# A projection split over two half cycles of the first batch, and two block turns moved behind an emptying, in a two-layer attention and experts kernel

## The reference, cut to what matters

```python
qz_u = qz @ ternary_factor_u.T * SCALE          # 16 channels x 64
qz_v = qz @ ternary_factor_v.T * SCALE
message_F = einsum('bcsr,bctr->bcst', qz_u, qz_v)
qh = sigmoid(message_F)
qh_v1 = einsum('bcst,bctr->bcsr', qh, qz_v)     # output 0
qh_v2 = einsum('bcst,bcsr->bctr', qh, qz_u)     # output 1
message_G = (qh_v1 @ ternary_factor_u + qh_v2 @ ternary_factor_v) * SCALE
```

## Time and profile before

| | |
|---|---|
| median of 3 runs | 1441.76 us (1440.23 to 1442.63) |
| the profiled execution's own time | 1442.26 us |
| its span in the trace | 1440.1 us (2.2 us lie around it) |
| granted TensorE clock, mean | 0.99 |
| half cycles of batch 0 | 154.9 to 288 us |
| batches 1 to 7 | 288 to 1387 us, some 157 us each |
| last second layer alone | 1387 to 1440 us |

### The profile page before, as it was taken

How to read it: one execution, slowest core, us unless ns; L and a number is a source line. 1 busy time by engine, 2 the same in 40 slices (tenths; PEclk the granted TensorE clock), 3 DMA queues, 4 the chain that set the end, 5 groups by cost and what they waited for, 6 DMA issues and landing times.

```text
span 1440.1 us, 24389 instructions
## 1 busy us (share of the span) xinstructions
PE 1379.7 (96%) x7814; PEld 788.6 (55%) x7814; DVE 897.1 (62%) x1546; ACT 697.7 (48%) x1077; POOL 44.7 (3%) x41
## 2 busy tenths in 40 slices
PE   5989899999999999999999999999999999999977
PEld 3556554455565555555655556555555555555544
DVE  7868544556656566566556565665655665656657
ACT  6556554454444553454535545445445444454431
POOL 4000400000000000000000000000000000000000
PEclk9999999999999999999999999999999999999988
DMA  6012122222112221111222112211122211222110
GB/s 211 1 31 68 37 37 30 30 38 31 26 26 35 36 31 29 33 32 29 30 31 35 32 26 30 39 33 28 24 37 38 30 26 24 35 30 30 27 26 8
DMA packets 298256, 50.66 MB, mean 35 GB/s; under 512 B 276192, under 2 KB 296416, under 8 KB 298112
## 3 DMA queue, kind: packets, MB, share of 16 engines
q1 hardware_dynamic: 297776, 47.29, 19.4%
q0 software_dynamic: 336, 1.64, 0.3%
HBM read 11.64 MB, written 4.19 MB: 11 GB/s over the span
## 4 chain that ended last, share of the span: by engine, by line
issue 85%; PE 2%; DVE 1%; POOL 1%; ACT 0%; POOLq 0%; DVEq 0%
PE psum L1264 2%; DVE arena L925 0%; POOL v_w_hl L614 0%; POOL u_w_hl L614 0%; DVE arena L923 0%; DVE arena L931 0%; POOL rstd_s L629 0%; ACT arena L1035 0%; PE psum L1626 0%; DVE xn_s L669 0%; POOL u_w_hl L611 0%; POOL v_w_hl L611 0%; POOL up_hl L614 0%; DVE x_all L940 0%; POOL gate_hl L611 0%
## 5 line engine op out<-in xcount | busy, mean ns | idle before, releaser
L1203 ACT ACTIVATE arena<-psum 128x1024 f32<-128x1024 f32 x504 | 477.0, 1031 | 611.0 <-PE psum L1264 604.0
L1264 PE MATMUL psum<-arena 128*64 128x512 f32 x2016 | 462.2, 601 | 4.8 <-ACT arena L1203 4.8
L1264 PEld LDWEIGHTS psum<-arena 128*64 128x64 f32 x2016 | 133.9, 137 | 264.8 <-issue 244.3
L1264 PE MATMUL psum<-v_parts,u_parts 64*128 64x512 f32 (+1 forms) x1568 | 208.3, 402 | 12.8 <-DVE o_hl L876 12.6
L1264 PE MATMUL psum<-u_parts,v_parts 64*128 64x512 f32 x1536 | 196.3, 399 | 4.0 <-issue 3.3
L1264 PEld LDWEIGHTS psum<-v_parts,u_parts 64*128 64x128 f32 (+1 forms) x1568 | 144.1, 185 | 101.3 <-issue 58.3
L1264 PEld LDWEIGHTS psum<-u_parts,v_parts 64*128 64x128 f32 x1536 | 139.8, 184 | 84.1 <-issue 39.9
L874 DVE TENSOR_SCALAR o_hl<-psum,sums 128x512 fp32r<-128x512 f32 x126 | 93.5, 742 | 83.3 <-PE psum L1264 82.2
L876 DVE SCALAR_TENSOR_TENSOR o_hl<-psum,sums,o_hl 128x512 fp32r<-128x512 f32 x126 | 94.6, 751 | 4.5
L931 DVE TENSOR_TENSOR arena<-psum,arena 128x512 f32<-128x512 f32 x96 | 64.5, 689 | 50.4 <-PE psum L1264 48.4
L1148 ACT ACTIVATE arena<-psum 128x512 f32<-128x512 f32 x128 | 77.3, 628 | 18.3 <-PE psum L1264 18.3
(11 more groups left out here) (214 smaller groups left out, 1515.2 us busy)
## 6 DMA issues: line engine op xcount, KB each, us to landing
arena<-blocks SPq DMA_DIRECT2D x1008, 32.0 KB, 2.0
x_all<-in_x SPq DMA_DIRECT2D x4, 512.0 KB, 6.1
upper<-in_we SPq DMA_DIRECT2D x8, 256.0 KB, 2.7
expert_rows<-upper SPq DMA_DIRECT2D x16, 128.0 KB, 2.5
xn_s<-expert_rows SPq DMA_DIRECT2D x8, 256.0 KB, 2.9
out<-x_all SPq DMA_DIRECT2D x8, 256.0 KB, 2.8
arena<-in_e POOLq DMA_DIRECT2D x1, 896.0 KB, 6.5
arena<-in_wi POOLq DMA_DIRECT2D x1, 576.0 KB, 6.7
```

The lines of the kernel that those rows point to most:

```text
L1203: nc.scalar.activation(th_of(un), psum[:, at:at + 2], ACT.Tanh, scale=0.5 * FACTOR_SCALE ** 2).then_inc(s_th, 2)
L1264: return nc.tensor.matmul(out, lhsT, rhs, start=start, stop=stop)
```

## The change: what it does

Two things are changed. First, in batch 0 the projection `pj` (six matmuls in even half cycle `2j`, of both outputs of pair `j-1`) becomes two: `pj0` (three matmuls, output 0 of pair `j` itself) in odd half cycle `2j+1`, for pairs 1 to 6, and `pj1` (three matmuls, output 1 of pair `j-1`) in even half cycle `2j`, for pairs 2 to 7. Each has its own bank and its own `add_g`, so DVE adds 12 times in batch 0 where it added 6 times. The last pair of batch 0 is projected whole in batch 1, as before. Counts of semaphores follow (`projected_count`).

Second, from batch 1 on, `turn` of pairs 0 and 2 stands behind `evac_o` of the same even half cycle (0 and 4), not ahead of it.

```diff
+LATE_TURNS = (0, 2)
 def first_middle_of(h):
 
-    work = [w for w in MIDDLE[h] if w[0] in ("pu", "pv", "pj") and w != ("pj", 1)]
-    return work + [("sc", 0)] * (h == FIRST_SCATTER_HALF)
+    j = h // 2
+    if h % 2 == 0:
+        return [("pu", j), ("pv", j)] + [("pj1", j)] * (j > 1)
+    return [("pj0", j)] * (j < PAIRS - 1) + [("sc", 0)] * (h == FIRST_SCATTER_HALF)
+
+
+def projected_count(kind, g):
+
+    return g + PAIRS - 2 if kind == "pj" else g * 2 - (kind == "pj1")
...
+def summed_count(g, o):
+
+    if isinstance(g, int) and g < PAIRS:
+        return projected_count("pj1", g) if o else projected_count("pj0", g - 1)
+    return projected_count("pj", g)
...
-                    dve.wait_ge(s_pj_full, g)
+                    dve.wait_ge(s_pj_full, summed_count(g, o))
...
-                    if o == 0:
+                    late = second and j in LATE_TURNS
+                    if o == 0 and not late:
                         if not some_before:
                             for n in range(2):
                                 dve.wait_ge(s_ymv[n], 16 * E)
                         turn(i, j)
                     evac_o(g, j, o, some_before)
+                    if o == 0 and late:
+                        turn(i, j)
...
-            def project(g, j, bk):
-
-                pe.wait_ge(s_oe, g * 2)
-                was = (j - 1) % PAIRS
-                passes = [(o, a, b) for o in range(2) for a, b in ((0, 0), (0, 1), (1, 0))]
+            def project(kind, g, j, bk):
+
+                pe.wait_ge(s_oe, g * 2 + 1 if kind == "pj0" else g * 2)
+                of = j if kind == "pj0" else (j - 1) % PAIRS
+                outputs = {"pj": (0, 1), "pj0": (0,), "pj1": (1,)}[kind]
+                passes = [(o, a, b) for o in outputs for a, b in ((0, 0), (0, 1), (1, 0))]
...
-                        elif kind == "pj":
-                            if isinstance(i, int) and i == 0 and j == 2:
+                        elif kind in ("pj", "pj0", "pj1"):
+                            if kind == "pj0" and j == 1:
                                 pe.wait_ge(s_parts, 4)
```

More of the change, by code:

```diff
@@ L194 @@
 FIRST_USER_BEFORE = users_before(bank_order(list(FIRST_MIDDLE.items()), 0), False)
+def summed_count(g, o):
+    if isinstance(g, int) and g < PAIRS:
+        return projected_count("pj1", g) if o else projected_count("pj0", g - 1)
+    return projected_count("pj", g)
 def is_prep(work):
-    return work[0] in ("pu", "pv", "pj", "sc")
+    return work[0] in ("pu", "pv", "pj", "pj0", "pj1", "sc")
 def prep_index(g, k):
@@ L853, in _, with add_g @@
             expert_rows(E - 1, 1, E // 2 - 1)
-            def add_g(i, j):
-                bk = x_bank(("pj", j), not (isinstance(i, int) and i == 0))
-                dve.wait_ge(s_pj_full, i * PAIRS + j)
-                if isinstance(i, int) and i == 0 and j == 2:
+            def add_g(i, j, kind):
+                bk = x_bank((kind, j), kind == "pj")
+                dve.wait_ge(s_pj_full, projected_count(kind, i * PAIRS + j))
+                if (kind, j) == ("pj0", 1):
                     dve.wait_ge(s_pj_free, 1)
@@ L863, in add_g @@
                     before = gT[:]
-                if isinstance(i, int) and i == 0 and j == 3:
+                if (kind, j) == ("pj1", FIRST_SCATTER_HALF // 2 + 1):
                     dve.wait_ge(s_scf, 1)
@@ L980, in iteration @@
                 if not attn:
-                    add_g(i, 0)
+                    add_g(i, 0, "pj")
                     for step in L1_STEPS:
@@ L1000, in iteration @@
                             prep_v(g, (j + 1) % 2)
-                        elif work[0] == "pj":
-                            add_g(i, j)
+                        elif work[0] in ("pj", "pj0", "pj1"):
+                            add_g(i, j, work[0])
                         elif not is_prep(work) and second:
@@ L1489, in emptied @@
                     g = i * PAIRS + n
-                    if kind == "pj":
-                        pe.wait_ge(s_pj_free, g)
+                    if kind in ("pj", "pj0", "pj1"):
+                        pe.wait_ge(s_pj_free, projected_count(kind, g))
                     elif kind == "sc":
@@ L1532, in prep @@
                 ins.then_inc(s_prep_full, 1)
-            def project(g, j, bk):
-                pe.wait_ge(s_oe, g * 2)
-                was = (j - 1) % PAIRS
-                passes = [(o, a, b) for o in range(2) for a, b in ((0, 0), (0, 1), (1, 0))]
+            def project(kind, g, j, bk):
[3 more added lines that the diff above has]
+                passes = [(o, a, b) for o in outputs for a, b in ((0, 0), (0, 1), (1, 0))]
                 for n, (o, a, b) in enumerate(passes):
-                    ins = mm(bk[:], w_hl[o][:, a, was * D:(was + 1) * D], o_hl[:, o, b], n == 0, n == len(passes) - 1)
+                    ins = mm(bk[:], w_hl[o][:, a, of * D:(of + 1) * D], o_hl[:, o, b], n == 0, n == len(passes) - 1)
                 ins.then_inc(s_pj_full, 1)
@@ L1620, in l1 @@
                 if kind == "back":
-                    pe.wait_ge(s_pj_free, (L + 1) * PAIRS)
+                    pe.wait_ge(s_pj_free, projected_count("pj", (L + 1) * PAIRS))
                     for t in range(TB):
@@ L1693, in iteration @@
                             scatter(i, scatter_bank(i))
-                        elif kind == "pj":
-                            if isinstance(i, int) and i == 0 and j == 2:
+                        elif kind in ("pj", "pj0", "pj1"):
+                            if kind == "pj0" and j == 1:
                                 pe.wait_ge(s_parts, 4)
                             wait_x_bank(work, h, i, second)
-                            project(g, j, x_bank(work, second))
+                            project(kind, g, j, x_bank(work, second))
                         elif is_prep(work):
@@ L1718, in iteration @@
                 if not second:
-                    pe.wait_ge(s_pj_free, PAIRS - 1)
+                    pe.wait_ge(s_pj_free, projected_count("pj1", PAIRS - 1))
                     pe.wait_ge(s_prep_free, prep_index(PAIRS - 1, 2) + 1)
```

4 lines of the change are left out of this document (2 added, 2 removed).

## The result

The changed kernel takes 1432.52 us (median of 4 runs, 1431.63 to 1434.75), the kernel before 1441.91 beside it: ratio 0.9939, 95% interval 0.9924 to 0.9955. The forecast was 1431.2, with a range of 1428.6 to 1434.6.

The account below looks back on a forecast made before the run. PE, busy in 96% of the span, was taken to bound the kernel. The terms -9.1 + 0.3 + 0.3 - 2.8 + 0.1 + 0.6 = -10.6 took 1441.76 to 1431.2 us, range 1428.6 to 1434.6.

Parts of the forecast that it names:

- Eleven waits for the emptying, -9.1: Batches 1 to 7, half cycles 1 and 5: PE's eleven waits vanish once the turn stands behind the emptying, -9.1 us.
- Cover of the turn, 0: DVE's idle time behind the emptying hides the moved turn, cost 0; without cover each turn would cost up to 1.24.
- Token moves at late turns, +0.3: Moves start 1.5 later, usually 0.9 left before PE needs them; slow sets cost +0.3 for all, between 0 and 3.5.
- rival (a): Token moves are late often: up to +1.8 in batch 0 and +3.2 at late turns, 1436.2, likelier 1433.7; chance 0.14.
- ACT's tanh in half cycle 5, 0: PE's `weighted` in half cycle 5 finds the third tanh done with 0.12 to spare: no wait, cost 0.
- rival (b): ACT's tanh and the emptying behind it take back 0.4 in each of 7 batches, 2.8 together: 1434.0; chance 0.08.
- Register computations, +0.3: Ten more register computations of 32 ns in three rounds of the loop: 1.0 at most, taken as +0.3.
- The split, -2.8: Batch 0: six even half cycles lose three matmuls each, -4.2; half cycles 3 and 5 pay +1.4; net -2.8.
- The emptying's reserve, +0.1: Batch 0, even half cycles: PE comes 0.70 earlier, using 0.5 of its 0.5 to 0.6 reserve; +0.1, up to 0.6.
- pair 5's moves, +0.6: Batch 0: PE needs pair 5's token moves 1.4 sooner with 0.87 to spare; +0.6, between 0 and 2.4.
- (d): No change: the emptying wait becomes an equal token wait, with landing 1.8 later at every late turn; 1440 to 1442; chance 0.04.
- (e): Slower: late sets land more than 1.7 later than usual; with 2.0 at all 14, 15.4 paid, 1446.6; chance 0.03.

Follow-up runs that it names:

- e3: The changed kernel with only the turn of pair 0 late (split kept): 1435.92 us, ratio 0.9964 to the kernel before.
- e4: The changed kernel with only the turn of pair 2 late (split kept): 1435.83 us, ratio 0.9968 to the kernel before.
- e10: The kernel before with the split projection alone, only from half cycle 7 of batch 0 on, no late turns: 1440.26 us, ratio 0.9990.
- e5: The changed kernel with 12 of the 16 token moves for pairs 0 and 2, output not the reference's: 1429.47 us, ratio 0.9916 to the kernel before.
- e6: The changed kernel with the late turns' last four token moves issued from ACT's queue: 1428.49 us, ratio 0.9914 to the kernel before.
- group 3: Runs on where the split's gain stays: split from half cycle 7 with and without two queues, two queues without split, two queues again; 1429.07, 1440.26, 1433.37, 1431.30 us.
- e12: The same kernel as e6 (moves on two queues) run again on another chip: 1431.30 us, ratio 0.9923 to the kernel before.
- e11: The kernel before with late turns of pairs 0 and 2, their last four moves on ACT's queue, no split: 1433.37 us, ratio 0.9940.
- e8: The changed kernel again with no edit, on another chip: 1434.06 us, ratio 0.9949 to the kernel before.
- e2: The kernel before with the late turns of pairs 0 and 2 alone, projection whole: 1433.99 us, ratio 0.9956.

## Why the prediction was right, and which term was wrong

- **Eleven waits for the emptying, -9.1.** Right, to the last one: none is left in batches 1 to 7, and each pair gives back its own (e3: 5.5 left of pair 2, e4: 3.6 left of pair 0). Half cycles 1 and 5 shortened by 10.5. Of the 1.4 beyond the waits 0.9 are in half cycle 1, whose length also moves without late turns (batch 6: 9.36 before, 8.98 in e10), and 0.5 in half cycle 5; where they come from stays open.
- **Cover of the turn, 0.** Right: DVE still idles behind both late turns in all seven batches (0.59 to 0.95 and 2.41 to 2.46).
- **Token moves at late turns, +0.3.** Wrong in size, this is the term that failed: 2.7 by the waits, 3.4 by the half cycles. The reserve of 0.9 was right to a tenth, and the 3.4 lie just under the upper bound of 3.5. The step that failed is "Few of the other late sets were slow, so I take +0.3 for all": I took the length of a set in the trace before as that of the same set moved by 1.5 against PE's work. Even there four of the fourteen were 0.6 to 1.1 over the usual (batches 1, 4, 6 and 7), three of these far into the loop, so rival (a)'s remark that both slow sets shown are from batches 0 and 1 says little: the trace had others. The slow sets are those that a fetch of instructions falls into, and in five batches one stood just behind the old landing. Before, two of pair 2's seven sets met one; now all seven do, and six of them are waited for. That is rival (a) in its mechanism: of the 3.5 that it gives the late turns (0.3 in the sum and 3.2 more) 2.7 came, of its 1.8 in batch 0 nothing. That the waits come from the late landing is shown (e4, e5, e6). That the fetch makes the landing late rests on the sets with and without one in fourteen traces; no run moved the fetch alone.
- **ACT's tanh in half cycle 5, 0, and rival (b).** A little too low: where the forecast left 0.12 to spare, PE now stands 0.09 to 0.16 for a tanh ahead of `weighted` in each of the seven half cycles 5, 0.8 together. It is not the 0.4 in each of rival (b).
- **Register computations, +0.3.** Not seen as a wait; the waits for "issue" at the edges of batches 3 and 5 went from 3.0 to 3.4, and from 2.7 to 3.8 over all the kernels tried, without an order that fits the change.
- **The split, -2.8.** -3.1 in the trace of the changed kernel and -2.8 in that of the split alone, but both by luck of the clock: half cycle 3's cost, forecast at 0.7, was hidden by a stretch of half clock of 3.4 us in place of 6.8. At the same 6.8 it costs 0.9, and the split gives 1.8 to 2.3 (group 3). The runs allow that: 0.7 (means, split alone), 0.5 (means, the changed kernel's 9 runs against late only, each against its own before), 2.9 (two queues with, 9 runs, against without). Each is uncertain by about 1. On one chip, e12 against e11, it is 1.6 (means) or 2.1 (medians).
- **The emptying's reserve, +0.1, and pair 5's moves, +0.6.** Together 0.2 in this trace: one wait in half cycle 12, of 0.2, for pair 5's moves. In the second trace of the same kernel (e8) the wait is 0.4 and in half cycle 14, for pair 6's.
- **(d), (e).** Not borne out: no late set came more than 1.7 over the usual 11.8 (13.45 in e4 is the longest, 13.39 in the changed kernel), and 1.7 at each of the 14 was the point from which they decide.

Sum by what was measured: -9.1 - 1.4 + 3.4 + 0.4 - 3.1, and another 0.35 won ahead of half cycle 2 of batch 0, which no edit touches, is -10.2 of the -10.3 in the spans. The 2.4 to 3.1 by which the moves' term was too small were in part made up in this one trace by the 1.4 in half cycles 1 and 5, the shorter stretch of half clock and the 0.35, so that it came out so close is luck. The median, 1.3 above the forecast, and the second measurement, 1434.06, show more of the miss.

## What to carry to other kernels

A reserve read off a trace ("lands 0.9 before it is needed") holds only for the place where it was read: look at what stands right behind it in time, here the next instruction fetch on the DMA engines, before work is moved there. If a wait is removed by delaying a transfer's source, shorten the transfer in the same change, for instance by a second queue on an engine that idles there. That was worth 5.6 us on one chip, but 3.5 over all runs (means of 9 against 9, each against its own before), which is what the traces show in half cycles 2 and 6, and only 1.2 without the split (e11 against e2). And a gain of 2 us in 1440 is read from the trace half cycle by half cycle, against traces with the same stretches of half clock; the runs blur it.

## What the hardware showed unexpectedly

- One 16 KB fetch of instructions held a DMA engine for 1.0 us, and the 32 KB move beside it landed in 3.1 in place of 2.0. Sets of 16 moves without any fetch took 11.74 to 11.85 in 311 cases of 311.
- After a wait of 1.89 at a batch's edge the granted clock was 0.50 for 3.4 us, which cost 1.55. In the kernel before a wait of 1.77 at that edge (half cycle 15 of batch 3) had no such stretch behind it; in e12 the edge of batches 5 and 6 had one.
- Behind the same wait of 3.5 in batch 0, half cycle 3 took from 10.36 (late only, no low clock) over 12.84 to 13.85 (both with three matmuls more), from trace to trace.
